# Band mask of each slot's first pair of heads written into PSUM by ScalarE, attended rows on two banks, and a few steps moved in the slot table

## The chip, the cores and the metric

One core of one Trainium2 chip. The time is device microseconds (us) of one execution. PE is the TensorE, DVE the VectorE, ACT the ScalarE, POOL the GpSimd, SP the engine that here only issues DMAs. Each has its own queue and works it in order; they meet at semaphores.

## The reference

A transformer block on x of 8 x 512 x 256 (batch, tokens, features), in float32:

```python
h = _layernorm(x) * (1 + ca) + sa
x = x + ga * _L0_attn_ref(h, w_qkv, b_qkv, w_out, b_out)   # 16 heads of 16, band |i - j| <= 64
h = _layernorm(x) * (1 + cb) + sb
x = x + gb * _L0_ffn_ref(h, gate_w, gate_bias, w_gate, w_up, w_down)   # 64 experts, 8 per token
# in the attention:
scores = jnp.einsum('bhqd,bhkd->bhqk', q, k) * SCALE + mask
attn = jax.nn.softmax(scores, axis=-1)
out = jnp.einsum('bhqk,bhkd->bhqd', attn, v)
```

The feed-forward part routes every token to 8 of 64 experts (capacity 256 each) and adds the weighted expert outputs.

## The kernel before

**Stages.** After a start, the attended part runs over 8 batches (0 to 7), then a tail routes the last batch, then 64 experts run, then the sums are put together. Each batch takes 20 slots: slot = 5g + u, where g counts four groups of four heads ("quads") and u five blocks of 128 keys. u = 0 and u = 4 are the ends of the band, 128 queries wide for each head; u = 1 to 3 are 256 wide.

**A slot on PE.** For two pairs of heads p = 0, 1, `scoresT` writes transposed scores into bank `bST[m % 2]`, m = 10g + 2u + p, so p = 0 is always bank scoresT0 and p = 1 always scoresT1. It begins with a product of an identity and the band mask (L1002, `start=True`), on which two products of keys and queries are added (L1006). Between them stand `fills` (L980), the scores of a later quad for the row maxima; none stand in slots with u = 3. Then `values` (L1022) multiplies the attended weights of the slot before. `turn_m`, in slots with u = 3, turns the maxima of the next quad; ACT copies them (L784) and sends them by DMA into the queries (`Qs<-MT`), which the first `scoresT` of the next quad waits for.

**The others.** ACT takes `exp` of each bank (`exps`, L779). DVE takes the row maxima (`maxima`, L1249, 4 instructions in each slot that has fills).

**Stage work** is put into the slots by a table, `AT`, a number for each step. At a slot of batch b three batches are in work: b itself, the one before (`prev`: its output product, second norm, routing) and the next ones (their first norm, projections and splitting; a negative number n means slot 20 + n of two batches earlier). The steps that matter here:

- `load_x` (SP, slot 6): the DMA of x of batch b + 2 into the single buffer `xt`. SP's queue has ahead of it, in this batch, storing the split projections (`store`, L435, slots 1 and 3), zeroing (L406) and 12 loads of the stacked operands (`stack`, L353, slot 4).
- `stats` (DVE, slots 9 and 10): the norm statistics of `xt`, two halves (`a_stats`, L1213 and L1217). The first half waits for the DMA of `load_x`.
- `onT`, `op`, `x1` (PE and ACT, PE, DVE): turn the attended rows of `prev`, multiply by `wo`, add to x (L1281 and L1284). x plus the bias comes from POOL (`c_xb`, L613, slot 2).
- `stats2`, `c_rstd`, `xhat`, `norm2`, `h2T`: statistics of that sum (DVE), their roots (POOL, slot 5), normalising (ACT, L805, slot 6), scale and shift (DVE, two instructions of L1303, both in slot 7), turned by PE in slots 8 and 9 (L1070), each into the same bank stageC.
- POOL besides splits the projections (L596, L599, L604), scales the sum by the output gate (`c_xs`, L619, slot 11) and, from batch 2 on, sends 32 groups of rows to the experts' slots by indirect DMA (L642).

On DVE the order inside one slot is: maxima, split_m, route, key, norm_o, `a_stats`, `a_mod`, `a_v`, `c_x1`, `c_stats`, `c_norm`.

Of the kernel before, what the change touches and what calls it, by code (L numbers as in the profile page):

```python
# [29 lines left out]
P = 128  # L30
# [33 lines left out]
    exp=10 * QUADS, pv=10 * QUADS, oTs=QUADS, oTp=QUADS, rec=QUADS, on=QUADS,  # L64
# [61 lines left out]
def build(nc, x, w_qkv, b_qkv, w_out, b_out, gate_w, gate_bias, w_gate, w_up, w_down, c, wmod, out):  # L126
    with ExitStack() as ctx:
# [613 lines left out]
        def _(act):  # L741
# [78 lines left out]
            def body(prev, now, nxt):  # L820
                for slot in range(SLOTS):
# [16 lines left out]
                    for k in at("onT", slot) if prev else []:  # L838
                        c_onT(prev, k)
# [60 lines left out]
        def _(pe):  # L900
# [304 lines left out]
        def _(dve):  # L1205
# [224 lines left out]
            def body(prev, now, nxt):  # L1430
                for slot in range(SLOTS):
# [146 lines left out]
```

## Time and profile before

| | |
|---|---|
| time, median of 3 runs | 989.44 us (984.01 to 989.56) |
| the profiled execution: time, span | 989.2 us, 987.5 us |
| busy: PE, DVE, ACT, POOL | 73%, 55%, 38%, 65% of the span |
| attended slots | 52.3 to 588 us |
| tail, experts, final sums | 588 to 690, 690 to 946, 946 to 987.5 us |

The profile is one execution, and times in its rows are from the span's start. A row of windows has the stretch, its length, the busy time and count of instructions of PE, PE's weight loads, DVE, ACT and POOL, then the granted clock of TensorE as a share of 2.4 GHz, the busy share of the DMA engines and GB/s. In a timeline the brackets at a row's end give the idle time ahead of it and what ended it.

### The profile page before, as it was taken

How to read it: one execution, taken by the hardware profiler on the slowest of the kernel's cores; microseconds unless marked ns; L12 is line 12 of the kernel's file. 1: busy time of each engine (PE TensorE's matmuls, PEld its weight loads, DVE VectorE, ACT ScalarE, POOL GpSimd, SP SyncE). 2: the span in 40 equal slices, each digit the busy share in tenths (PEclk: the TensorE clock that was granted, in tenths of full speed). 3: DMA queues.
4: the chain of work that ended last, by engine and by line, in shares of the span. 5: the costliest groups of instructions: out<-in, count | busy, mean ns of one | idle time of the engine just before them, and what ended most of it. 6: DMA issues, size and time to landing. Idle time of an engine off the chain costs nothing.

```text
span 987.5 us, 15482 instructions
## 1 busy us (share of the span) xinstructions
PE 719.3 (73%) x4732; PEld 470.7 (48%) x4732; DVE 544.6 (55%) x1974; ACT 373.7 (38%) x827; POOL 643.2 (65%) x592
## 2 busy tenths in 40 slices
PE   4579998997997897989988861200899998888200
PEld 3235555554554564554455530200788777666100
DVE  3566569779869878778678772600222222222038
ACT  2135654544444455445444530000344333333100
POOL 5206332687786886886885656776388888887630
PEclk9879998998987998898898976555899999999755
DMA  8695996275466446534526379100999999898878
GB/s 306 162 341 159 333 336 189 82 251 180 172 202 227 151 157 212 181 101 162 172 97 201 115 227 282 37 5 4 247 277 276 263 231 159 162 161 182 216 211 332
DMA packets 165134, 191.60 MB, mean 194 GB/s; under 512 B 21497, under 2 KB 146581, under 8 KB 165052
## 3 DMA queue, kind: packets, MB, share of 16 engines
q1 hardware_dynamic: 128636, 134.27, 42.7%
q0 software_dynamic: 30720, 38.03, 18.8%
q10 hardware_dynamic: 5696, 18.30, 5.2%
q8 instruction: 39, 0.64, 0.3%
q14 instruction: 43, 0.35, 0.1%
HBM read 100.77 MB, written 110.67 MB: 214 GB/s over the span
## 4 chain that ended last, share of the span: by engine, by line
PE 36%; DVE 20%; POOL 15%; DMA 12%; issue 11%; SPq 3%; ACT 2%; POOLq 0%; DVEq 0%; ACTq 0%
POOL acc_d L725 8%; DMA acc_d<-ys,xg 7%; PE stageA L952 6%; POOL slots_d L642 5%; PE outT L1022 4%; PE scores L980 4%; PE scoresT L1181 4%; DVE junk L1249 4%; PE scoresT L1002 4%; PE scoresT L1006 3%; PE stageA L962 2%; DVE pairs L1313 2%; PE stageC L1077 2%; DVE sc L1313 1%; PE stageC L1059 1%
## 5 line engine op out<-in xcount | busy, mean ns | idle before, releaser
L642 POOL DMA_INDIRECT slots_d<-H,dest x256 | 259.1, 1012 | 95.0 <-issue 57.4
L725 POOL DMA_INDIRECT acc_d<-ys,xg x128 | 198.4, 1550 | 60.3 <-issue 29.8
L1249 DVE CUSTOM_DVE_ANT_0 junk<-scores,mask 128x256 bf16<-128x256 f32 x512 | 187.6, 419 | 76.1 <-PE scores L980 75.8
L779 ACT ACTIVATE PT<-scoresT 128x512 f32<-128x512 f32 (+1 forms) x320 | 152.8, 508 | 140.7 <-PE scoresT L1006 137.1
L1181 PE MATMUL scoresT<-xgT,wgu 128*128 128x256 f32 x512 | 127.6, 393 | 23.0 <-ACT xgT L873 22.8
L1002 PE MATMUL scoresT<-mask,identb 128*128 128x512 bf16 (+1 forms) x320 | 116.5, 364 | 19.8 <-DMA Qs<-MT 14.3
L980 PE MATMUL scores<-Ks,Qs 96*128 96x256 bf16 x512 | 108.5, 298 | 30.4 <-DVE mrowmax L1249 26.6
L1181 PEld LDWEIGHTS scoresT<-xgT,wgu 128*128 128x128 f32 x512 | 96.1, 194 | 48.3 <-ACT xgT L873 35.3
L1006 PE MATMUL scoresT<-Qs,Ks 98*128 98x256 bf16 (+1 forms) x640 | 117.1, 267 | 0.0
L1022 PE MATMUL outT<-PT,Va 128*32 128x256 f32 (+1 forms) x1280 | 94.9, 370 | 0.0
L596 POOL TENSOR_TENSOR r<-p,parts 128x512 f32<-128x512 f32 x32 | 39.3, 1227 | 78.7 <-ACT parts L771 77.2
L1006 PEld LDWEIGHTS scoresT<-Qs,Ks 98*128 98x128 bf16 x640 | 66.9, 104 | 41.7 <-issue 12.5
L1532 DVE COPY xgT<-stageA 128x256 f32<-128x256 f32 x32 | 13.6, 424 | 122.4 <-PE stageA L1169 122.4
L952 PE MATMUL stageA<-hT,wqkv 128*128 128x512 f32 x128 | 74.0, 707 | 3.4 <-ACT p L767 2.4
L980 PEld LDWEIGHTS scores<-Ks,Qs 96*128 96x128 bf16 x512 | 45.9, 104 | 43.8 <-DVE mrowmax L1249 34.9
L1169 PE MATMUL scores<-ident,xg 128*128 128x128 f32 x128 | 24.9, 277 | 52.0 <-DMA xg<-slots_d 52.0
L1002 PEld LDWEIGHTS scoresT<-mask,identb 128*128 128x128 bf16 x320 | 33.0, 103 | 48.1 <-DMA Qs<-MT 20.7
L1532 DVE COPY xgT<-stageC 128x256 f32<-128x256 f32 x32 | 13.6, 424 | 75.8 <-PE stageC L1169 75.8
L886 ACT ACTIVATE ys<-outT,xg 128x256 f32<-128x256 f32 x64 | 26.8, 470 | 63.1 <-DMA acc_d<-ys,xg 56.6
L873 ACT ACTIVATE xgT<-scores 128x256 f32<-128x256 f32 x64 | 24.7, 386 | 67.3 <-PE scores L1169 67.3
L962 PE MATMUL stageA<-wqkv,hT 128*128 128x256 f32 x160 | 41.0, 395 | 9.0 <-DVE Va L1232 8.1
L886 ACT ACTIVATE ys<-turns,xg 128x256 f32<-128x256 f32 x64 | 26.8, 470 | 53.5 <-DMA acc_d<-ys,xg 47.0
(195 smaller groups left out, 1179.5 us busy)
## 6 DMA issues: line engine op xcount, KB each, us to landing
xg<-slots_d SPq DMA_DIRECT2D x64, 324.0 KB, 4.4
slots_d<-blank ACTq DMA_DIRECT2D x26, 648.0 KB, 5.1
parts_d<-parts SPq DMA_DIRECT2D x32, 384.0 KB, 2.7
Qs<-parts_d SPq DMA_DIRECT2D x96, 128.0 KB
Ks<-parts_d SPq DMA_DIRECT2D x90, 128.0 KB
acc_d<-zero SPq DMA_DIRECT2D x32, 272.0 KB
wgu<-L_ffn_w_gate_dram SPq DMA_DIRECT2D x64, 128.0 KB, 3.2
wgu<-L_ffn_w_up_dram SPq DMA_DIRECT2D x64, 128.0 KB, 3.3
```

Source lines behind the costliest of these rows:

```text
L642: pool.indirect_dma_start(out=slots_d[:, :], in_=H2[bt.par][:, t, :], in_offset=None, out_offset=bass.IndirectOffsetOnAxis(ap=dest[bt.par] ...
L725: pool.indirect_dma_start(out=acc_d[ACC[e]][:, :], in_=ys[e % NY][:, h, :], in_offset=None, out_offset=bass.IndirectOffsetOnAxis(ap=xg[e % ...
L779: sc_.activation(PT[m % NPT][:, :, 0:w], src, ACT.Exp).then_inc(sems["exp"], 1)
L886: sc_.activation(ys[e % NY][:, h, :], yb[:, h * D:(h + 1) * D], ACT.Copy, scale=xg[e % NX][:, h, D + e:D + e + 1]).then_inc(mo["yc"], 1)
L952: last = mm(bA[:, :], wqkv[:, k, f * P:(f + 1) * P], hT[:, k, BAND:BAND + S], start=(k == 0), stop=(k == C - 1))
L962: last = mm(bA[:, i * D:(i + 1) * D], hT[:, k, u * P:(u + 1) * P], wqkv[:, k, 2 * D:3 * D], start=(k == 0), stop=(k == C - 1))
L980: last = mm(bS[n % 2][:, i * 2 * P:(i + 1) * 2 * P], q[0:MROW, h, t * P:(t + 1) * P], kk[0:MROW, h, t * P:(t + 2) * P], start=True, stop=True)
L1002: mm(bST[m % 2][:, 0:2 * (hi - lo)].rearrange("p (h q) -> p h q", h=2), identb[:], half.unsqueeze(1).to_broadcast([P, 2, hi - lo]), start= ...
L1006: last = mm(bST[m % 2][:, i * (hi - lo):(i + 1) * (hi - lo)], kk[0:KROWS, h, u * P:(u + 1) * P], q[0:KROWS, h, lo:hi], start=False, stop=T ...
L1022: last = mm(bO[32 * j:32 * j + 32, lo:hi], Va[bt.par][rows, u, HQ * g + j, :], PT[m % NPT][rows, i, 0:hi - lo], start=(u == 0), stop=(u == ...
L1181: last = mm(bST[par][:, a * CAP:(a + 1) * CAP], wgu[e % NW][:, a, k, :], xgT[par][:, k, :], start=(k == 0), stop=(k == C - 1))
L1249: ins = v.tensor_tensor_reduce(out=junk[:, i, :], in0=bS[n % 2][:, i * 2 * P:(i + 1) * 2 * P], in1=mask[:, edge, :], scale=1.0, scalar=TAK ...
```

## The change

Three edits come together.

1. **Seeds.** For p = 0 the mask product is gone. ACT writes the band mask (a bf16 tile in SBUF, broadcast over two heads) into bank scoresT0 by a copy (`seed`), right behind the `exp` that emptied the bank and ahead of the `exp` of p = 1. The first product of keys and queries of the next slot waits for the semaphore `seed` in place of `exp`, and adds to what is there. A product of the identity over the whole bank, in the start, comes ahead of the first seed. p = 1 keeps its mask product.
2. **Two banks.** `onT`, `op` and `x1` of a batch that is not the last use stageC for the first half and stageA for the second (`PAIR`), so the waits of the second half for the first are gone. `a_proj` of the third projection, and `onT`, have waits in their place.
3. **The table.** `onT` moves from slots 2, 3 to 2, 2; `op` from 4, 5 to 3, 3; `x1` from 4, 5 to 3, 4; `stats2` from 5, 5 to 4, 5; `norm2` from 7, 7 to 7, 8; the first half of `stats` from slot 9 to slot 8.

```diff
-    load_x=(-14,), stats=(-11, -10), a_rstd=(-9,), ...
+    load_x=(-14,), stats=(-12, -10), a_rstd=(-9,), ...
-    xb=(2,), onT=(2, 3), op=(4, 5), x1=(4, 5), ..., stats2=(5, 5), c_rstd=(5,), xhat=(6,), norm2=(7, 7),
+    xb=(2,), onT=(2, 2), op=(3, 3), x1=(3, 4), ..., stats2=(4, 5), c_rstd=(5,), xhat=(6,), norm2=(7, 8),
...
+        PAIR = (bC, bA)
...
+            def seed(bt, m):
+                u = m % 10 // 2
+                half = mask[:, 1, P:2 * P] if u == 0 else mask[:, 1, 0:P] if u == U - 1 else mask[:, 1, :]
+                w = P if u in (0, U - 1) else 2 * P
+                if bt.b > 0 or m >= 2:
+                    after(act, "exp", bt, m - 1)
+                sc_.activation(bST[m % 2][:, 0:2 * w].rearrange("p (h q) -> p h q", h=2),
+                               half.unsqueeze(1).to_broadcast([P, 2, w]), ACT.Copy).then_inc(sems["seed"], 1)
...
                 sc_.activation(PT[m % NPT][:, :, 0:w], src, ACT.Exp).then_inc(sems["exp"], 1)
+                if p == 0 and m + 2 < 10 * QUADS:
+                    seed(bt, m + 2)
+                elif p == 0 and bt.b < B - 1:
+                    seed(batch(bt.b + 1), 0)
...
+                if j == 2 and bt.b >= 2:
+                    after(pe, "t1", batch(bt.b - 2), 2)
...
-                after(pe, "exp", bt, m - 1)
...
-                mm(bST[m % 2][:, 0:2 * (hi - lo)].rearrange("p (h q) -> p h q", h=2), identb[:],
-                   half.unsqueeze(1).to_broadcast([P, 2, hi - lo]), start=True, stop=False, skip_group_check=True)
+                if p == 0:
+                    after(pe, "seed", bt, m // 2 + 1)
+                else:
+                    after(pe, "exp", bt, m - 1)
...
+                    mm(bST[1][:, 0:2 * (hi - lo)].rearrange("p (h q) -> p h q", h=2), identb[:],
+                       half.unsqueeze(1).to_broadcast([P, 2, hi - lo]), start=True, stop=False, skip_group_check=True)
...
-                if bank is bC and k == 0:
+                if bt.b < B - 1 and bank is bC:
                     after(pe, "key", bt, -1)
-                elif bank is bC:
-                    after(pe, "onT", bt, k)
+                elif bt.b < B - 2:
+                    after(pe, "p32", batch(bt.b + 2), 2)
...
-                if bank is bC:
-                    after(pe, "t1", bt, n)
...
+            mm(bST[0][:, :], identb[:], mask[:, 0:2, :], start=True, stop=True).then_inc(s_pe0, 1)
```

Line numbers of the kernel after are higher: L1303 before is L1328 after, L1213 is L1238, L1249 is L1274, L1002 is L1025, L1006 is L1029, L1059 is L1082.

DVE, slots 7 to 9 of batch 3 (the same in batches 1 to 5). Before: the two steps of the second norm, then the maxima of slot 9, then the statistics of `xt`.

```order
L1303 TENSOR_TENSOR H2_0<-H2_0,mr 128x4x256 [waits s_xn2]
L1303 TENSOR_TENSOR H2_0<-H2_0,mr 128x4x256 [waits s_h2]
L1249 ISA junk,mrowmax<-scores0,mask 128x256 [waits s_smax,s_m2,s_Sp]
L1249 ISA mrowmax 128x1
L1249 ISA junk,mrowmax<-scores0,mask 128x256 [waits s_smax]
L1249 ISA mrowmax 128x1
L1249 ISA junk,mrowmax<-scores1,mask 128x256 [waits s_smax,s_Sp]
L1249 ISA mrowmax 128x1
L1249 ISA junk,mrowmax<-scores1,mask 128x256 [waits s_smax]
L1249 ISA mrowmax 128x1
L1213 BN_STATS stats<-xt 128x6 [waits x_loaded_odd]
```

After, the same place:

```order
L1328 TENSOR_TENSOR H2_0<-H2_0,mr 128x4x256 [waits s_xn2]
L1238 BN_STATS stats<-xt 128x6 [waits x_loaded_odd]
L1238 BN_STATS stats<-xt 128x6
L1242 BN_AGGR mv<-stats 128x2 [waits s_stats,s_rstd]
L1242 BN_AGGR mv<-stats 128x2 [waits s_stats]
L1328 TENSOR_TENSOR H2_0<-H2_0,mr 128x4x256 [waits s_h2]
L1274 ISA junk,mrowmax<-scores0,mask 128x256 [waits s_smax,s_m2,s_Sp]
L1274 ISA mrowmax 128x1
```

The first half of the statistics, with its wait for the load of x, now stands between the two steps of the second norm and ahead of the maxima of slot 9. PE's first `h2T` needs both steps of the norm.

DVE, slots 4 and 5 of batch 1, where `x1` and `stats2` stand. Before:

```order
L1281 TENSOR_TENSOR x1<-stageC,mr 128x512 [waits s_xb,s_op]
L1284 TENSOR_TENSOR x1<-x1,xc 128x512 [waits s_t1]
L1249 ISA junk,mrowmax<-scores0,mask 128x256 [waits s_smax,s_Sp]
L1249 ISA mrowmax 128x1
L1249 ISA junk,mrowmax<-scores0,mask 128x256 [waits s_smax]
L1249 ISA mrowmax 128x1
L1249 ISA junk,mrowmax<-scores1,mask 128x256 [waits s_smax,s_Sp]
L1249 ISA mrowmax 128x1
L1249 ISA junk,mrowmax<-scores1,mask 128x256 [waits s_smax]
L1249 ISA mrowmax 128x1
L1281 TENSOR_TENSOR x1<-stageC,mr 128x512 [waits s_xb,s_op]
L1284 TENSOR_TENSOR x1<-x1,xc 128x512 [waits s_t1]
```

After, from the end of slot 2 on:

```order
L1285 SCALAR_TENSOR_TENSOR M2<-mrowmax,M2 128x16 [waits s_m2]
L1306 TENSOR_TENSOR x1<-stageC,mr 128x512 [waits s_xb,s_op]
L1309 TENSOR_TENSOR x1<-x1,xc 128x512 [waits s_t1]
L1274 ISA junk,mrowmax<-scores0,mask 128x256 [waits s_smax,s_m2,s_Sp]
L1274 ISA mrowmax 128x1
L1274 ISA junk,mrowmax<-scores0,mask 128x256 [waits s_smax]
L1274 ISA mrowmax 128x1
L1274 ISA junk,mrowmax<-scores1,mask 128x256 [waits s_smax,s_Sp]
L1274 ISA mrowmax 128x1
L1274 ISA junk,mrowmax<-scores1,mask 128x256 [waits s_smax]
L1274 ISA mrowmax 128x1
L1306 TENSOR_TENSOR x1<-stageA,mr 128x512 [waits s_xb,s_op]
```

The first `x1` now comes ahead of the maxima of slot 4, where it came behind them.

ACT, slot 3 of batch 0. Before:

```order
L779 ACTIVATE PT2<-scoresT0 128x512 [waits s_pv,s_STp]
L779 ACTIVATE PT3<-scoresT1 128x512 [waits s_pv,s_STp]
L784 ACTIVATE MT<-turns 32x128 [waits s_mrow_ld,s_mTp]
L786 DMA Qs0<-MT 2x16x128 [waits s_mT]
L757 ACTIVATE hT<-stageA,mcol 128x512 [waits s_vp,s_mcol,s_hTp]
```

After:

```order
L791 ACTIVATE PT2<-scoresT0 128x512 [waits s_pv,s_STp]
L782 ACTIVATE scoresT0<-mask 128x256 [waits s_exp]
L791 ACTIVATE PT3<-scoresT1 128x512 [waits s_pv,s_STp]
L800 ACTIVATE MT<-turns 32x128 [waits s_mrow_ld,s_mTp]
L802 DMA Qs0<-MT 2x16x128 [waits s_mT]
```

A copy of the mask stands between the two `exp` of every slot; its width is that of the next slot.

## Rows read from the trace of the kernel before

**Rows 1.** Windows of batches 0 and 4 (columns as explained above).

```profile
52.32:116.89 64.57, 60.06 (x429) 31.82 (x429) 38.67 (x172) 34.55 (x70) 19.36 (x22) 0.94 0.78 274
...
322.96:391.95 68.99, 60.24 (x461) 36.18 (x460) 56.31 (x225) 34.45 (x71) 55.47 (x56) 0.93 0.56 184
```

**Rows 2.** Timeline of PE, slot 15 of batch 4.

```profile
371.92 0.28 PE L1002 MATMUL scoresT<-mask,identb 128*128 128x256 bf16 x1 [1.77 <-DMA Qs<-MT]
...
375.87 0.61 PE L980 MATMUL scores<-Ks,Qs 96*128 96x256 bf16 x2 [3.54 <-DVE mrowmax L1249]
```

**Rows 3.** Timeline of DVE, slot 12 of batch 4.

```profile
368.32 3.94 DVE L1313 TENSOR_TENSOR pairs<-pairs 128x64 f32<-128x64 f32 x4
```

**Rows 4.** Timeline of POOL, slot 11 of batch 4.

```profile
369.81 2.36 POOL L619 TENSOR_TENSOR x<-x,mr 128x1024 f32<-128x1024 f32 x1
```

**Rows 5.** The page, costliest groups: the mask product.

```profile
L1002 PE MATMUL scoresT<-mask,identb 128*128 128x512 bf16 (+1 forms) x320 | 116.5, 364 | 19.8 <-DMA Qs<-MT 14.3
```

**Rows 6.** Timeline of PE, slots 10 and 12 of batch 4: start us, us, what.

```profile
355.83 0.27 PE L1002 MATMUL scoresT<-mask,identb 128*128 128x256 bf16 x1
355.94 0.28 PE L1006 MATMUL scoresT<-Qs,Ks 98*128 98x128 bf16 x2
...
363.03 0.38 PE L1002 MATMUL scoresT<-mask,identb 128*128 128x512 bf16 x1
363.25 0.38 PE L1006 MATMUL scoresT<-Qs,Ks 98*128 98x256 bf16 x2
```

**Rows 7.** Timeline of ACT, a step that reads SBUF.

```profile
319.97 0.63 ACT L771 ACTIVATE parts<-p 128x512 bf16<-128x512 f32 x1
```

**Rows 8.** Timeline of PE, slot 1 of batch 4.

```profile
324.84 0.39 PE L1002 MATMUL scoresT<-mask,identb 128*128 128x512 bf16 x1 [0.47 <-ACT PT L779]
```

**Rows 9.** Timeline of the SP queue, batch 4.

```profile
345.75 3.86 SPq L353 DMA_DIRECT2D Ks<-parts_d  x6
349.65 0.64 SPq L416 DMA_DIRECT2D xt<-L_attn_x_dram  x1
```

**Rows 10.** Timeline of DVE, slots 7 to 9 of batch 4.

```profile
347.13 2.48 DVE L1303 TENSOR_TENSOR H<-H,mr 128x1024 f32<-128x1024 f32 x2 [0.76 <-ACT H L805]
...
355.75 0.75 DVE L1213 BATCH_NORM_STATS2 stats<-xt 128x6 f32<-128x256 f32 x2 [1.63 <-DMA xt<-L_attn_x_dram]
356.42 0.30 DVE L1217 BATCH_NORM_AGGREGATE mv<-stats 128x2 f32<-128x6 f32 x2
```

**Rows 11.** Timeline of PE, slots 8 and 9 of batch 4.

```profile
351.58 0.60 PE L1070 MATMUL stageC<-ident,H 128*128 128x128 f32 x4
352.01 0.27 PE L1002 MATMUL scoresT<-mask,identb 128*128 128x256 bf16 x1
```

**Rows 12.** Timeline of PE, slot 8 of batches 1 and 5 (first and last).

```profile
143.38 0.60 PE L1070 MATMUL stageC<-ident,H 128*128 128x128 f32 x4
...
422.10 0.60 PE L1070 MATMUL stageC<-ident,H 128*128 128x128 f32 x4
```

**Rows 13.** Timeline of DVE, slot 9 of batches 1 and 5 (first and last).

```profile
147.79 0.75 DVE L1213 BATCH_NORM_STATS2 stats<-xt 128x6 f32<-128x256 f32 x2 [1.86 <-DMA xt<-L_attn_x_dram]
...
424.57 0.75 DVE L1213 BATCH_NORM_STATS2 stats<-xt 128x6 f32<-128x256 f32 x2
```

**Rows 14.** Timeline of POOL, slot 19 of batch 3 to slot 2 of batch 4.

```profile
320.69 1.15 POOL L596 TENSOR_TENSOR r<-p,parts 128x512 f32<-128x512 f32 x1 [1.71 <-ACT parts L771]
...
332.76 2.36 POOL L613 TENSOR_TENSOR xc<-xc,gbo 128x1024 f32<-128x1024 f32 x1
...
336.31 1.17 POOL L604 TENSOR_TENSOR parts<-r,parts 128x512 bf16<-128x512 f32 x1
```

**Rows 15.** Timeline of DVE, slots 4 and 5 of batch 4.

```profile
336.03 2.01 DVE L1284 TENSOR_TENSOR x<-x,xc 128x512 f32<-128x512 f32 x1
...
340.06 0.69 DVE L1284 TENSOR_TENSOR x<-x,xc 128x512 f32<-128x512 f32 x1
```

**Rows 16.** Window: slots 15 and 16 of batch 4, behind a stop of PE.

```profile
375.90:382.00 6.10, 6.10 (x40) 3.62 (x41) 5.83 (x29) 2.17 (x4) 4.04 (x6) 0.56 0.69 224
```

More of the change, by code:

```diff
@@ L63 @@
     lpart=4, vp=3, v=3, Sp=8 * QUADS, smax=2 * 8 * QUADS, m2=2 * QUADS, mTp=QUADS, mT=QUADS, STp=10 * QUADS,
-    exp=10 * QUADS, pv=10 * QUADS, oTs=QUADS, oTp=QUADS, rec=QUADS, on=QUADS,
+    exp=10 * QUADS, seed=5 * QUADS, pv=10 * QUADS, oTs=QUADS, oTp=QUADS, rec=QUADS, on=QUADS,
     onTp=C, onT=C, op=2, t1=2, xb=2, x1=2, xs=1, stats2=T, aggr2=T, rstd2=4, xn2=T, h2=2, h2Tp=C, h2T=C,
@@ L72 @@
 AT = dict(
-    load_x=(-14,), stats=(-11, -10), a_rstd=(-9,), a_norm=(-6,), a_mod=(-9,), hT=(-4, -3), proj=(-2, -1, 7, 8),
+    load_x=(-14,), stats=(-12, -10), a_rstd=(-9,), a_norm=(-6,), a_mod=(-9,), hT=(-4, -3), proj=(-2, -1, 7, 8),
     split=(-1, 0, 0, 1, 1, 2, 8, 8, 9, 9, 10, 10), store=(1, 3, 10, 11), stack=(4, 12), v=(9, 11, 12),
-    xb=(2,), onT=(2, 3), op=(4, 5), x1=(4, 5), x1_store=(10,), xs=(11,), stats2=(5, 5), c_rstd=(5,), xhat=(6,), norm2=(7, 7),
+    xb=(2,), onT=(2, 2), op=(3, 3), x1=(3, 4), x1_store=(10,), xs=(11,), stats2=(4, 5), c_rstd=(5,), xhat=(6,), norm2=(7, 8),
     h2T=(8, 9), lg=(10,), route=(11, 12, 12, 13, 13, 14, 15, 15, 16, 17, 18, 18), cnt=(18,), key=(19,), zero=(3,),
@@ L440, in load_stack @@
                 if bt.b == 1:
-                    sp.wait_ge(s_pe0, 6)
+                    sp.wait_ge(s_pe0, 7)
                 if bt.b >= 2:
@@ L838, in body @@
                     for k in at("onT", slot) if prev else []:
-                        c_onT(prev, k)
+                        c_onT(prev, k, PAIR[k])
                     for _ in at("xhat", slot) if prev else []:
@@ L856, in _ @@
             load_side(act, batch(0), 0, 1)
+            act.wait_ge(s_pe0, 5)
+            seed(batch(0), 0)
             take_mT(batch(0), 0)
@@ L998, in scoresT @@
                 m = 10 * g + 2 * u + p
-                after(pe, "exp", bt, m - 1)
-                half = mask[:, 1, P:2 * P] if u == 0 else mask[:, 1, 0:P] if u == U - 1 else mask[:, 1, :]
-                mm(bST[m % 2][:, 0:2 * (hi - lo)].rearrange("p (h q) -> p h q", h=2), identb[:],
-                   half.unsqueeze(1).to_broadcast([P, 2, hi - lo]), start=True, stop=False, skip_group_check=True)
+                if p == 0:
+                    after(pe, "seed", bt, m // 2 + 1)
+                else:
+                    after(pe, "exp", bt, m - 1)
+                    half = mask[:, 1, P:2 * P] if u == 0 else mask[:, 1, 0:P] if u == U - 1 else mask[:, 1, :]
+                    mm(bST[1][:, 0:2 * (hi - lo)].rearrange("p (h q) -> p h q", h=2), identb[:],
+                       half.unsqueeze(1).to_broadcast([P, 2, hi - lo]), start=True, stop=False, skip_group_check=True)
                 for i in range(2):
@@ L1043, in c_onT @@
                 after(pe, "on", bt, QUADS)
-                if bank is bC and k == 0:
+                if bt.b < B - 1 and bank is bC:
                     after(pe, "key", bt, -1)
-                elif bank is bC:
-                    after(pe, "onT", bt, k)
+                elif bt.b < B - 2:
+                    after(pe, "p32", batch(bt.b + 2), 2)
+                elif bt.b == B - 2:
+                    after(pe, "v", batch(B), 0)
                 for t in range(T):
@@ L1114, in body @@
                     for k in at("onT", slot) if prev else []:
-                        c_onT(prev, k)
+                        c_onT(prev, k, PAIR[k])
                     for n in at("op", slot) if prev else []:
-                        c_op(prev, n)
+                        c_op(prev, n, PAIR[n])
                     for k in at("h2T", slot) if prev else []:
@@ L1411, in mod_gates @@
                 if part == 0:
-                    dve.wait_ge(s_pe0, 6)
+                    dve.wait_ge(s_pe0, 7)
                     v.tensor_copy(gates[:, 1, 0, :], bC[0:B, 0:D]).then_inc(s_v1, 1)
@@ L1452, in body @@
                     for n in at("x1", slot) if prev else []:
-                        c_x1(prev, n)
+                        c_x1(prev, n, PAIR[n])
                     for half in at("stats2", slot) if prev else []:
```

## The prediction

> **What bounds the kernel now.** I read the windows first, one for each attended batch. Batch 0, which has no second norm, no routing and no sends, takes 64.57 us of which PE is busy 60.06; batch 4, a full one, takes 68.99 with PE busy 60.24, DVE 56.31 and POOL 55.47 [rows 1]. POOL's sends have some 0.3 us between them that don't count as busy, so three in-order engines are nearly full and hand work to each other. Behind the attended slots come the tail and the experts. Neither is touched by the change, and both begin when the slots end, so the whole question is by how much the eight batches grow or shrink.
>
> Then I read the timeline of one full batch, engine by engine, to see who is late where. In batch 4 PE stands longest in slot 15: 1.77 us for the DMA of the maxima, then 3.54 us for DVE [rows 2]. DVE was late because four small `pairs` steps took 3.94 us together [rows 3] while POOL worked on `c_xs` for 2.36 us from 369.81 [rows 4].
>
> **What the seeds take away.** 160 of the 320 mask products go [rows 5]. A busy time of 0.38 us is not their price, since products overlap: the next one starts 0.22 us behind a wide one and 0.11 behind a narrow one [rows 6]. 96 wide and 64 narrow ones make 96 x 0.22 + 64 x 0.11 = 28 us of PE at full clock, 3.5 us in a batch. That is all there is to gain, and it comes only where PE is what the others wait for.
>
> **What they add.** A seed is a copy on ACT from SBUF. The nearest row is the 128x512 copy of L771, 0.63 us [rows 7]; a narrow one I take at half to two thirds of it. ACT is 34.45 us busy in 68.99 [rows 1], so 20 seeds of about 0.55, 11 us, fit beside its other work. What counts is latency: p = 0 of the next slot now waits for `exp` and a seed, and `exp` of p = 1 comes one seed later. Where PE already waits for ACT, as in slot 1 of batch 4 (0.47 us [rows 8]), p = 0 starts 0.6 us later and saves 0.22: a loss of 0.4. That is about one place in a batch. In slots with stage work behind them the seed is long done. Bounds for all seeds together: from 0 to 0.4 x 20 slots x 8 batches = 64 us; I take 0.4 in a batch, since the row shows one such place, and count it against the products below.
>
> **The table: one step decides.** `stats` of batch b + 2 moves from slot 9 to slot 8. Its load is not earlier: SP issued it at 349.65, right behind the twelve stack loads [rows 9]. Before, DVE finished both steps of the second norm at 347.13 + 2.48 = 349.61, did the maxima of slot 9, and then still had to wait 1.63 us for the load until 355.75 [rows 10]. After, the order is: first step of the norm, statistics, second step, maxima of slot 9. DVE therefore stands in slot 8 until 355.75; two statistics and their aggregates take until 356.65, the second step of the norm 1.24 (half of 2.48), so it is done at 357.9 [rows 10]. PE's first `h2T` needs it and started at 351.58, with slot 9 right behind at 352.01 [rows 11]. In batch 4 PE is held 357.9 - 351.6 = 6.3 us, and nothing else is queued on PE ahead of it.
>
> The same holds in batches 1 to 5, which have both a second norm and a batch + 2. In batch 1: 147.79 + 2.13 - 143.38 = 6.5 us; in batch 5: 424.57 + 2.13 - 422.10 = 4.6 us, at most, since there DVE came behind the load [rows 12, 13]. Batches 2 and 3 lie between, at 5.7 and 5.0. Sum of the five: 28 us. Batch 0 has no second norm and its load is there in time; batches 6 and 7 have no such statistics.
>
> Could what the change saves bring the load forward? It is tied to POOL, not to PE. POOL starts the splits of a batch when ACT hands over the first projection at 320.69, works without a gap worth the name through `c_xb` (332.76) and on to the split of 336.31 to 337.48 [rows 14]; the store, the zeroing and the twelve loads of SP follow back to back until 349.65 [rows 9]. From 320.69 to the landing it is 35 us, whatever PE does between. This also means that what PE saves in slots 19 to 8 of these batches is covered, and that what the new place of `x1` costs is covered too.
>
> **What `x1` costs.** The sum x1 needs `c_xb`, done at 335.12 [rows 14]. DVE now reaches it in slot 3 with the maxima of slot 4 queued behind, four of some 0.35. So after 335.12 DVE has 1.4 us more to do before the statistics of slot 5. In batches 1 to 5 the load hides that; in 6 and 7 it costs up to 1.4 each, against masks of 3.5 each.
>
> **Shared port.** DVE's addition of two SBUF tiles took 2.01 us at 336.03 and 0.69 at 340.06 [rows 15]; the first lay across POOL's split of 336.31 [rows 14]. The Trainium skill ("SBUF — State Buffer", section "SBUF: two separate sides") says that a DVE instruction with two SBUF inputs and a GpSimd one hold the shared pair for their whole length in turn. By that rule a norm step that meets a split would wait for all of it, which would make the sum up to 5 x 1.2 longer, 1020; the trace agrees in that the addition ended 0.56 us behind the end of that split. Without the rule: the second step of the norm, in its new place at 356.65, may take longer by as much as the addition did, 1.3 us. That is 0 to 1.3 in each of five batches, 0 to 6.5; I take 0 for the sum, since POOL's sends stand between its splits, and keep 6 for the range.
>
> **The clock.** In the stretch of 6.10 us behind PE's stop of 3.54 us, PE was busy all through at a granted clock of 0.56 [rows 2, 16], so 6.10 x 0.44 = 2.7 us were lost against full clock. The hold in slot 8 is longer than that stop and ends in slots 9 and 10, where PE, not DVE, sets the pace. Bounds 0 and 2.7; I take 2 in each of five batches: +10.
>
> **What comes back.** PE's two stops in slot 15 of batch 4 make 5.3 us [rows 2]. They arise because POOL lags and its long instructions fall on DVE's small ones [rows 3, 4]. POOL goes on while PE is held, so its lag shrinks by the hold, and `c_xs` then falls beside DVE's slot 11. I take 1.5 us back in each of batches 2 to 5: -6. Bounds 0 and the whole 5.3 in each.
>
> **The sum,** against the profiled execution, 989.2 us: hold +28; clock +10; stops -6; batch 0, where PE sets the pace, 3.5 less the seeds' latency, -3; mask products in slots 9 to 19 of batches 1 to 5, of which DVE, busy without a gap from slot 11, lets through 0.5 each, -2.5; batches 6 and 7, -2. Together +24.5: 1014 us. The profiled execution is the median of the runs shown to 0.2 us, so it stands for that too. The forecast's own range: without the clock term and with twice as much back from the stops, 998; with 2.7 of clock, the port and nothing back, 1029.
>
> **The rivals.**
> - **PE's relief counts in full and the hold does not.** It would need the load to be there before DVE gets to slot 8, by 6 us. For it: 28 us of products, twice that where the clock is 0.56. Against it: the wait of 1.63 us that DVE already had a slot later [rows 10]. It turns at a landing ahead of 349.6 in batch 4. With 16 to 20 us of the 28 it gives about 971. 8 in 100.
> - **The hold is given back later.** Had the stops of 5.3 us gone altogether in all five batches (27 us, of which I counted 6), the sum would be +24.5 - 21 = +3.5: 993. For it: DVE, which is late there, gets 6 us of standing in which POOL runs ahead. Against it: DVE stands too, so its own queue is no shorter, and its work from slot 11 on stays. 15 in 100.
> - **ACT joins in.** Seeds that delay both the next p = 0 and the `exp` of p = 1 in many short slots, 0.2 us over 100 slots, add 20: about 1034. For it: five engines in lockstep. Against it: ACT stands idle half of each batch. 11 in 100.
> - The edit does what it says: the products are gone from the order of PE. What it may not do is relieve anything, which is inside the forecast.
>
> **How the numbers follow.** Forecast (998 to 1029) 66 in 100, the three rivals 8, 15 and 11. The range of 990 to 1032 holds nearly all of the forecast, most of the second rival and half of the third, 8 in 10 together. Over 1% (9.9 us, about what a measurement of this kernel can tell from no change) slower: the third, nearly all of the forecast, 77 in 100. Within 1%: 15. Faster by more: 8.
>
> **What would show it.** In the profile after: DVE's first statistics of `xt` between the two steps of the second norm in batches 1 to 5, with 5 to 7 us of idle time before it that the load's DMA ended; PE idle ahead of L1093 by about as much; a granted clock near 0.5 in slots 9 and 10; a batch of some 74 us in place of 69 to 71, and batch 0 near 61.5. If those idle times are under 2 us, the forecast is wrong at its root. If they are there but the batch is under 71 us, the stops in slot 15 went with them.

## The result and the profile after

The changed kernel takes 1027.87 us (median of 4 runs, 1020.44 to 1028.69), the kernel before, run beside it, 986.73 (983.3 to 989.56). The ratio is 1.0402 with a 95% interval of 1.0336 to 1.0467: slower by 4%. The forecast was 1014, with a range of 990 to 1032.

The page of the kernel after, its span and its first part (busy time, share of the span, instructions), and two of its costliest groups:

```profile
span 1026.9 us, 15317 instructions
...
PE 735.7 (72%) x4572; PEld 473.2 (46%) x4573; DVE 543.8 (53%) x1974; ACT 450.2 (44%) x987; POOL 646.2 (63%) x592
...
L782 ACT ACTIVATE scoresT<-mask 128x512 f32<-128x512 bf16 (+1 forms) x160 | 82.5, 516 | 13.1 <-PE stageC L936 8.1
...
L1025 PE MATMUL scoresT<-mask,identb 128*128 128x512 bf16 (+1 forms) x160 | 65.7, 411 | 0.2
```

The edit did what it says: 160 mask products are left of 320 [rows 5], and ACT has 160 more instructions. PE is nevertheless busy longer than before (735.7 against 719.3 us), because what is left runs at a lower clock, 0.82 over the span against 0.86: one of the remaining mask products takes 411 ns on average, before 364 [rows 5]. The windows of batches 0 and 4 (columns as in [rows 1]):

```profile
50.23:116.31 66.08, 59.20 (x408) 30.33 (x409) 39.12 (x172) 43.84 (x90) 19.12 (x22) 0.91 0.75 268
345.69:423.64 77.95, 63.72 (x441) 36.94 (x440) 56.40 (x224) 43.99 (x91) 56.45 (x56) 0.85 0.49 163
```

Batch 4 is 9 us longer than its 68.99 [rows 1], of which only 3.5 are busy time of PE. Batch 0 is 1.5 us longer, where it should have been 3 shorter. The eight batches took 64.57, 64.92, 69.70, 71.45, 68.99, 71.49, 67.33 and 56.71 us before (the last one up to the end of its last `values`); after, 66.08, 73.48, 77.38, 78.52, 77.95, 75.98, 67.89 and 60.99. So nearly all of the loss, 37 of 39 us, lies in batches 1 to 5, where the forecast had put it. Batch 7 is 4.3 us longer, and what stands before batch 0 and behind batch 7 is 3.7 us shorter.

Where in the batch? The timeline of DVE, slots 7 and 8 of batch 4, answers to [rows 10]:

```profile
371.03 1.22 DVE L1328 TENSOR_TENSOR H<-H,mr 128x1024 f32<-128x1024 f32 x1
379.50 0.75 DVE L1238 BATCH_NORM_STATS2 stats<-xt 128x6 f32<-128x256 f32 x2 [7.25 <-DMA xt<-L_attn_x_dram]
380.17 0.30 DVE L1242 BATCH_NORM_AGGREGATE mv<-stats 128x2 f32<-128x6 f32 x2
380.39 1.19 DVE L1328 TENSOR_TENSOR H<-H,mr 128x1024 f32<-128x1024 f32 x1
```

DVE has half of the norm behind it, stands 7.25 us for the load of x, takes the statistics, and only then does the other half. In batches 1, 2, 3 and 5 it stands 5.04, 5.66, 5.42 and 3.03 us at the same place. PE, same stretch (it answers to [rows 11]):

```profile
375.13 1.94 PE L972 MATMUL stageA<-hT,wqkv 128*128 128x512 f32 x4
381.63 1.12 PE L1093 MATMUL stageC<-ident,H 128*128 128x128 f32 x4 [4.56 <-DVE H L1328]
```

PE's first `h2T` waits 4.56 us for that other half, and everything behind it with it. Once released it runs at a low clock: four transposes take 1.12 us where they took 0.60 [rows 11]. The load was where the forecast had it. SP's queue and the POOL step that starts the batch's splits (it answers to [rows 9, 14]):

```profile
343.52 1.15 POOL L598 TENSOR_TENSOR r<-p,parts 128x512 f32<-128x512 f32 x1 [1.47 <-ACT parts L773]
```

```profile
369.52 3.85 SPq L355 DMA_DIRECT2D Ks<-parts_d  x6
373.42 0.62 SPq L418 DMA_DIRECT2D xt<-L_attn_x_dram  x1
```

From 343.52 to the landing at 379.50 it is 36.0 us; before, 320.69 to 355.75, 35.1. Nothing that PE saved brought the load forward.

Two further readings speak of the seeds and of slot 15. PE in slots 1, 12, 15 and 16 of batch 4 (answers to [rows 2, 8]):

```profile
348.19 0.39 PE L1029 MATMUL scoresT<-Qs,Ks 98*128 98x256 bf16 x2 [1.21 <-ACT scoresT L782]
...
400.63 2.07 PE L982 MATMUL stageA<-wqkv,hT 128*128 128x256 f32 x4 [3.65 <-DVE Va L1257]
...
407.61 0.28 PE L1029 MATMUL scoresT<-Qs,Ks 98*128 98x128 bf16 x2 [1.55 <-DMA Qs<-MT]
409.79 0.39 PE L1029 MATMUL scoresT<-Qs,Ks 98*128 98x256 bf16 x2 [0.81 <-ACT scoresT L782]
```

Slot 1 now waits 1.21 us for a seed where it waited 0.47 for the exponentials [rows 8]. In slot 15 the stop of 3.54 us for DVE [rows 2] is gone; what is left is the wait for the maxima's DMA. But slot 12 has a stop of 3.65 us for DVE's `Va`, where before it was 0.88. DVE and POOL show where both come from:

```profile
393.77 3.26 DVE L1338 TENSOR_SCALAR ex<-ex 128x256 f32<-128x256 f32 x1
...
403.00 1.01 DVE L1338 TENSOR_TENSOR pairs<-pairs 128x64 f32<-128x64 f32 x4
```

```profile
394.51 2.36 POOL L621 TENSOR_TENSOR x<-x,mr 128x1024 f32<-128x1024 f32 x1
```

POOL's `c_xs` now ends 6 us ahead of the small `pairs` steps, which take 1.01 us together. Before, the two lay on each other and the same four steps took 3.94 us, from 368.32 to 372.26, while `c_xs` ran from 369.81 to 372.17 [rows 3, 4]. Now `c_xs`, from 394.51 to 396.87, lies on another step of DVE instead: `ex`, 0.29 us at 361.65 before, takes 3.26 and ends at 397.03. It stands in DVE's order ahead of `Va`, for which PE waits in slot 12. So in batch 4 the stop moved from slot 15 to slot 12. Over batches 1 to 5 slot 12 is 8.9 us longer than before and slots 15 and 16 are 10.0 shorter.

### The profile page after: what moved, and what is told of

It reads as the page before. It is cut to its first block, busy times and chain, and to the rows that moved or that the text cites. A ratio compares the mean times of both kernels' runs of the same rounds, so it can differ in the third digit from the quotient of the medians.

```text
span 1026.9 us, 15317 instructions
## 1 busy us (share of the span) xinstructions
PE 735.7 (72%) x4572; PEld 473.2 (46%) x4573; DVE 543.8 (53%) x1974; ACT 450.2 (44%) x987; POOL 646.2 (63%) x592
## 4 chain that ended last, share of the span: by engine, by line
PE 29%; DVE 17%; DMA 16%; POOL 16%; issue 11%; SPq 7%; ACT 4%; ACTq 0%; POOLq 0%; DVEq 0%
DMA acc_d<-ys,xg 9%; POOL acc_d L727 6%; SPq L355 6%; POOL slots_d L644 5%; DMA xt<-L_attn_x_dram 4%; PE outT L1045 3%; PE scoresT L1206 3%; PE scoresT L1029 3%; PE stageA L972 3%; DVE junk L1274 3%; PE scores L1000 3%; PE stageA L982 2%; PE stageC L1100 2%; PE scoresT L1025 2%; DVE sc L1338 2%
## 5 line engine op out<-in xcount | busy, mean ns | idle before, releaser
L1274 DVE CUSTOM_DVE_ANT_0 junk<-scores,mask 128x256 bf16<-128x256 f32 x512 | 189.2, 420 | 75.7 <-PE scores L1000 73.6
L791 ACT ACTIVATE PT<-scoresT 128x512 f32<-128x512 f32 (+1 forms) x320 | 160.5, 502 | 123.2 <-PE scoresT L1029 118.8
L1029 PE MATMUL scoresT<-Qs,Ks 98*128 98x256 bf16 (+1 forms) x640 | 130.2, 291 | 29.1 <-DMA Qs<-MT 15.5
L1000 PE MATMUL scores<-Ks,Qs 96*128 96x256 bf16 x512 | 116.7, 316 | 23.6 <-DVE mrowmax L1274 22.2
L1029 PEld LDWEIGHTS scoresT<-Qs,Ks 98*128 98x128 bf16 x640 | 64.6, 111 | 93.6 <-issue 34.8
L1045 PE MATMUL outT<-PT,Va 128*32 128x256 f32 (+1 forms) x1280 | 105.3, 407 | 0.0
L598 POOL TENSOR_TENSOR r<-p,parts 128x512 f32<-128x512 f32 x32 | 39.9, 1247 | 83.0 <-ACT parts L773 80.8
L782 ACT ACTIVATE scoresT<-mask 128x512 f32<-128x512 bf16 (+1 forms) x160 | 82.5, 516 | 13.1 <-PE stageC L936 8.1
L1557 DVE COPY xgT<-stageA 128x256 f32<-128x256 f32 x32 | 13.6, 425 | 122.1 <-PE stageA L1194 122.1
L972 PE MATMUL stageA<-hT,wqkv 128*128 128x512 f32 x128 | 68.8, 663 | 3.4 <-ACT p L769 2.4
L1000 PEld LDWEIGHTS scores<-Ks,Qs 96*128 96x128 bf16 x512 | 49.2, 111 | 40.4 <-DVE mrowmax L1274 31.1
L1025 PE MATMUL scoresT<-mask,identb 128*128 128x512 bf16 (+1 forms) x160 | 65.7, 411 | 0.2
L982 PE MATMUL stageA<-wqkv,hT 128*128 128x256 f32 x160 | 47.9, 446 | 17.9 <-DVE Va L1257 17.0
L1557 DVE COPY xgT<-stageC 128x256 f32<-128x256 f32 x32 | 13.6, 425 | 76.2 <-PE stageC L1194 76.2
```

Of the source, the lines that this page charges most:

```text
L782: sc_.activation(bST[m % 2][:, 0:2 * w].rearrange("p (h q) -> p h q", h=2), half.unsqueeze(1).to_broadcast([P, 2, w]), ACT.Copy).then_inc( ...
L982: last = mm(bA[:, i * D:(i + 1) * D], hT[:, k, u * P:(u + 1) * P], wqkv[:, k, 2 * D:3 * D], start=(k == 0), stop=(k == C - 1))
L1000: last = mm(bS[n % 2][:, i * 2 * P:(i + 1) * 2 * P], q[0:MROW, h, t * P:(t + 1) * P], kk[0:MROW, h, t * P:(t + 2) * P], start=True, stop=True)
L1025: mm(bST[1][:, 0:2 * (hi - lo)].rearrange("p (h q) -> p h q", h=2), identb[:], half.unsqueeze(1).to_broadcast([P, 2, hi - lo]), start=True ...
L1029: last = mm(bST[m % 2][:, i * (hi - lo):(i + 1) * (hi - lo)], kk[0:KROWS, h, u * P:(u + 1) * P], q[0:KROWS, h, lo:hi], start=False, stop=T ...
L1045: last = mm(bO[32 * j:32 * j + 32, lo:hi], Va[bt.par][rows, u, HQ * g + j, :], PT[m % NPT][rows, i, 0:hi - lo], start=(u == 0), stop=(u == ...
```

## The experiments

The theory on the stand was the hold: a late load in front of the norm's second step. Its rival: the seeds' latency on ACT, since slot 1 and batch 0 looked worse than forecast. All ratios are against runs of the kernel before made beside them on the same chip (medians 988.6 us for experiments 1 to 4, 988.2 for 5 to 8, 987.8 for 9 to 11). A difference between two experiments is one of medians and carries the uncertainty of both; the intervals are 2 to 6 us either way.

**1. Statistics back in slot 9.**

```diff
-    load_x=(-14,), stats=(-12, -10),
+    load_x=(-14,), stats=(-11, -10),
```

> The changed kernel with one number of the table put back: the first two statistics of a batch stand in slot 9 again, behind both steps of the second norm. Seeds, two banks and the rest of the table stay. If the wait for the load on DVE in slot 8 carries the loss (the traces: batches 1 to 5 are 37 us longer in all, DVE stands 5.04, 5.66, 5.42, 7.25 and 3.03 us in slot 8), PE's waits there go and 25 us or more of the 41 between the two kernels come back: 985 to 1003. If the seeds' latency on ACT carries it (slot 1 waits 1.21 us for a seed in place of 0.47 for the exponentials; batch 0, which has no such hold, is 1.5 us longer where it should be 3 shorter), at most 14 come back: 1013 or more.

Measured: 1003.86 us, ratio 1.0168 (1.0127 to 1.0209). One number of a table gives 24 us back. The hold is the largest part, but 15 us are left that it doesn't explain.

**2. The load two slots earlier instead.**

```diff
-    load_x=(-14,), stats=(-12, -10),
+    load_x=(-16,), stats=(-12, -10),
```

> The changed kernel with the load of x two slots earlier in SP's order, ahead of the stack loads; the statistics stay in slot 8. If the late load is the cause, DVE finds its tile there, the hold goes and the time is 985 to 1003, as with the statistics in slot 9, and perhaps below it, since DVE has the statistics behind it sooner. If the place of the statistics itself costs (their own DVE time ahead of the norm's second step, 0.9 us), or the seeds do, it stays at 1010 or more. A load ahead of the stack loads could also make these late and show up as a wait in slots 12 to 15 for the maxima's DMA.

Measured: 1003.24 us, ratio 1.0177 (1.0129 to 1.0225), the same as experiment 1. The timeline of DVE, slot 8 of batch 4:

```profile
356.49 1.22 DVE L1328 TENSOR_TENSOR H<-H,mr 128x1024 f32<-128x1024 f32 x1
357.62 0.74 DVE L1238 BATCH_NORM_STATS2 stats<-xt 128x6 f32<-128x256 f32 x2
358.50 1.19 DVE L1328 TENSOR_TENSOR H<-H,mr 128x1024 f32<-128x1024 f32 x1
```

The order is that of the changed kernel and there is no wait. So the statistics ahead of the norm cost nothing that shows; the wait for their load does. The time lies just above the upper end of what I expected, as that of experiment 1 did, again with 15 us unexplained.

**3. No seeds, the rest of the change kept.**

```diff
-                if p == 0 and m + 2 < 10 * QUADS:
-                    seed(bt, m + 2)
...
-                if p == 0:
-                    after(pe, "seed", bt, m // 2 + 1)
-                else:
-                    after(pe, "exp", bt, m - 1)
-                    ... mm(bST[1][...], identb[:], half, start=True)
+                after(pe, "exp", bt, m - 1)
+                ... mm(bST[m % 2][...], identb[:], half, start=True)
```

> The changed kernel with the mask again as a product for both pairs of heads, no seeds on ACT; two banks and the new table stay. If the hold carries the loss, it stays slower than before by 25 us or more: 1010 to 1028, and slot 8 of batch 4 still waits about 4 us for DVE. If the seeds' latency carries it, 27 us or more come back: 1000 or less.

Measured: 1023.51 us, ratio 1.0369 (1.0327 to 1.0411). The rival falls as the main cause: without any seed the kernel is 4 us faster (not clear of noise), not 27. PE waits 2.40 us for `H` in slot 8 of batch 4, less than the 4 I expected, and 16.7 us in batches 1 to 5 together, against 16.2 in the changed kernel.

**4. Seeds alone** (one bank, old table).

```diff
-        PAIR = (bC, bA)
+        PAIR = (bC, bC)
-    stats=(-12, -10), ... onT=(2, 2), op=(3, 3), x1=(3, 4), stats2=(4, 5), norm2=(7, 8)
+    stats=(-11, -10), ... onT=(2, 3), op=(4, 5), x1=(4, 5), stats2=(5, 5), norm2=(7, 7)
... and the waits of `a_proj`, `onT` and `op` as before
```

> The kernel before with the seeds alone: one bank and the old table. If the hold carries the loss, this is within 10 us of the kernel before, 978 to 998, with slot 8 of batch 4 free of a wait for DVE. If the seeds carry it, it is 1010 or more. Batch 0 should be about 66 us long, as in the changed kernel, against 64.6 before, if the seeds are what lengthens it.

Measured: 996.02 us, ratio 1.009 (1.0057 to 1.0123). The seeds are a loss by themselves, 7.4 us. Batch 0 took 64.2 us in its profiled run, not 66, so that part of my reading of the changed kernel was wrong. What the loss looks like, in slots 1 and 2 of batch 5, on ACT and on PE:

```profile
394.75 0.36 ACT L791 ACTIVATE PT<-scoresT 128x256 f32<-128x256 f32 x1
395.14 0.60 ACT L782 ACTIVATE scoresT<-mask 128x512 f32<-128x512 bf16 x1
```

```profile
395.80 0.39 PE L1027 MATMUL scoresT<-Qs,Ks 98*128 98x256 bf16 x2 [1.22 <-ACT scoresT L782]
```

The exponentials come late, behind the projection's two copies, and the seed of 0.60 us stands behind them. The windows from slot 1 of batch 5 on, seeds alone (slots 1 and 2) and then the kernel before (the same and 1.1 us of slot 3), with us, PE busy, PEclk, DMA share, GB/s:

```profile
395.80:402.80 7.00, 6.83 (x42) 0.62 0.29 104
```

```profile
393.93:399.80 5.87, 5.87 (x54) 1.00 0.35 124
```

In this stretch the granted clock is 0.62, between the two levels of 1.2 and 2.4 GHz; before, at the same place, behind a stop of 0.47 us for the exponentials, it is 1.00. In batch 4 slots 1 and 2 took 2.38 and 2.27 us behind the same wait, in batch 5 2.86 and 4.17: the wait doesn't lower the clock each time. Of PE's waits for seeds in this run, 15.8 us in 13 places, 13.6 are in slots 1 and 8; slots 3, 11 and 16 have one each, in batch 0.

**5. Two banks alone** (no seeds, statistics in slot 9).

```diff
 the edit of experiment 3, and
-    load_x=(-14,), stats=(-12, -10),
+    load_x=(-14,), stats=(-11, -10),
```

> The changed kernel without seeds and with the statistics in slot 9: what is left of the change is the pair of banks and the earlier places of onT, op, x1 and stats2. The seeds alone cost 7 us over the kernel before, and the changed kernel with the statistics in slot 9 costs 15. If the parts add up, this is 8 us slower than before, 993 to 1001. If the banks cost only where seeds delay PE too, it is within 4 us of before, 985 to 992.

Measured: 998.51 us, ratio 1.0093 (1.0058 to 1.0128). So the banks with their table cost something too when the hold is away. DVE in slots 3 and 4 of batch 4:

```profile
337.92 0.69 DVE L1297 TENSOR_TENSOR x<-stageC,mr 128x512 f32<-128x512 f32 x1 [4.24 <-POOL xc L615]
338.64 2.06 DVE L1300 TENSOR_TENSOR x<-x,xc 128x512 f32<-128x512 f32 x1
340.63 0.41 DVE L1265 CUSTOM_DVE_ANT_0 junk<-scores,mask 128x256 bf16<-128x256 f32 x1
```

And PE in slots 5 and 6:

```profile
341.45 0.39 PE L994 MATMUL scores<-Ks,Qs 96*128 96x256 bf16 x2 [1.59 <-DVE mrowmax L1265]
...
345.06 0.61 PE L994 MATMUL scores<-Ks,Qs 96*128 96x256 bf16 x2 [1.03 <-DVE mrowmax L1265]
```

`x1` now stands in DVE's order ahead of the maxima of slot 4. It needs `c_xb`, which POOL gives when it gives it, and DVE stands 4.24 us with maxima behind it that PE waits for. The waits of DVE over the whole run: for POOL's `xc` it is 29.8 us in 6 places. One of them, of 8.6 us, is in the tail, and the kernel before has one of 8.8 there; the other five, 21.2 us, are in the attended slots, where it has none.

```profile
DVE x L1297 <- POOL xc L615: 29.8, 6, 8.6
```

PE's own waits don't account for the 10 us. In slots 5 to 7 of batches 1 to 5 they make 14.3 us; before, 10.0, all in slot 7. But there are now two stops in a row, and the granted clock in these slots is 0.73 where it was 0.85. No run here separates the clock from the rest.

**6. The hold alone,** on the kernel before.

```diff
-    stats=(-11, -10), ... norm2=(7, 7)
+    stats=(-12, -10), ... norm2=(7, 8)
```

> The kernel before with the two numbers of the table that make the hold: first statistics in slot 8, second step of the second norm behind them. If the hold stands on its own feet, it costs here what it gave back there, 20 to 30 us: 1008 to 1020, with PE waiting 4 to 6 us in slot 8 of batches 1 to 5. If it took the earlier x1 and the seeds to bring it out, it is under 1000.

Measured: 1023.05 us, ratio 1.0349 (1.0288 to 1.0409). Two numbers, 35 us, 3 above the range that I expected. PE in slot 8 of batch 4, and its waits over the whole run (us in total, times, longest):

```profile
377.83 1.11 PE L1070 MATMUL stageC<-ident,H 128*128 128x128 f32 x4 [6.23 <-DVE H L1303]
```

```profile
PE stageC L1070 <- DVE H L1303: 28.5, 5, 6.6
```

The five waits are 6.57, 5.99, 4.56, 6.23 and 5.16 us. Slots 8 and 9 of these batches took 38.4 us in all before and 77.2 here; less the waits that leaves 10.3 us which PE spent longer on the same work, its clock being 0.81 in the stretch behind the wait:

```profile
377.83:386.50 8.67, 8.66 (x66) 0.81 0.26 93
```

The five batches together are 30.5 us longer (377.1 against 346.6), so 8 us came back. That is a difference of larger numbers. Slots 14 to 16 of the five batches are 24 us shorter (slot 15 of batch 4 took 1.79 us in place of 5.92), but slot 12 is 8.5 us longer and slots 17 and 18 are 5.9 longer.

Set beside experiment 3, which has the banks and their table on top of this hold, the two are the same: 1023.51 and 1023.05 us, ratios 1.0369 and 1.0349. With the hold in place the banks cost nothing that shows.

**7. Seeds in 16 of 20 slots,** on experiment 4.

```diff
+        APART = (1, 8, 11, 16)
...
             def seed(bt, m):
+                if m // 2 in APART:
+                    return
...
-                if p == 0:
+                if p == 0 and m // 2 not in APART:
...
```

> The kernel before with seeds in 16 of 20 slots: slots 1, 8, 11 and 16, where PE waited up to 1.2 us for one, have their product back. If those waits, and the clock of 0.7 behind the one in slot 1 (against 1.00 at the same place before), are what eats the products saved, this is 4 to 14 us below the seeds everywhere: 982 to 992, slots 1 and 2 again under 2.6 us in all batches. If the seeds cost by what ACT is late in all slots, it stays at 994 or more.

Measured: 989.87 us, ratio 1.0018 (0.9995 to 1.0041). With the products of the four bad places back the loss is gone, and slots 1 and 2 take 2.36 and 2.26 us in each of batches 1 to 6. No run took four other slots out for comparison. But there is no gain either, though 128 products are away, 64 wide and 64 narrow, by the pitches of [rows 6] 21 us of PE at full clock. The waits of PE, this kernel and then the kernel before:

```profile
PE scores L1000 <- DVE mrowmax L1274: 38.1, 22, 4.1
...
PE turns L1007 <- DVE M L1285: 14.7, 15, 3.4
...
PE stageA L982 <- DVE Va L1257: 9.6, 7, 2.1
```

```profile
PE scores L980 <- DVE mrowmax L1249: 26.6, 18, 3.9
...
PE turns L987 <- DVE M L1260: 11.9, 10, 3.6
...
PE stageA L962 <- DVE Va L1232: 8.1, 7, 1.9
```

PE waits 15.8 us more for DVE (62.4 against 46.6). By that estimate three quarters of the relief turned into waits for DVE.

**8. Both steps of the norm ahead of the late statistics.**

```diff
-    stats=(-12, -10), ... norm2=(7, 8)
+    stats=(-12, -10), ... norm2=(7, 7)
```

> The changed kernel with both steps of the second norm in slot 7, ahead of the statistics, which stay in slot 8 and wait there for the load as before. If the loss comes by way of the norm's second step, for which h2T and all of PE behind it wait, this is near the kernel with the statistics in slot 9: 1002 to 1012. If DVE's standing as such is what counts (the maxima of slot 9 behind it), it stays at 1018 or more.

Measured: 1001.2 us, ratio 1.0128 (1.0064 to 1.0191). DVE in slots 7 and 8 of batch 4, and PE's only wait for it in the next slots:

```profile
356.02 2.48 DVE L1328 TENSOR_TENSOR H<-H,mr 128x1024 f32<-128x1024 f32 x2
363.35 0.75 DVE L1238 BATCH_NORM_STATS2 stats<-xt 128x6 f32<-128x256 f32 x2 [4.85 <-DMA xt<-L_attn_x_dram]
```

```profile
365.12 0.39 PE L1000 MATMUL scores<-Ks,Qs 96*128 96x256 bf16 x2 [0.50 <-DVE mrowmax L1274]
```

DVE still stands 4.85 us for the same load, and it costs nothing that shows: experiment 1, where that wait is 0.21 us, took 1003.86. So the loss is not DVE's idle time but what was queued behind it, the one step that PE needs next.

**9. Two banks with `x1` where it was.**

```diff
 experiment 5, and
-    x1=(3, 4), stats2=(4, 5)
+    x1=(4, 5), stats2=(5, 5)
```

> The run with two banks alone (998.5), with x1 and its statistics back in slots 4 and 5; onT and op stay early, in two banks. If the loss of the banks comes from x1 ahead of the maxima of slot 4 (there DVE stood 4.24 us in batch 4 for POOL's xc, and PE 1.59 us for the maxima in slot 5), this is back at the kernel before: 984 to 992, and DVE's wait for POOL in slot 4 is under 2.5 us. If PE's own order costs (both op products in slot 3, 3.6 us in a row, ahead of the scores of the next slots), it stays at 995 or more.

Measured: 994.25 us, ratio 1.0059 (1.0033 to 1.0086). Neither: DVE's wait for POOL is back at 7.6 us in one place, but only some 4 of the 10 us came back, and the intervals of the two experiments overlap. PE's waits in slots 5 to 7 are as long as in experiment 5 (14.6 us in batches 1 to 5), at a clock of 0.82 in place of 0.73. So the share of `x1` is not clear of noise, and the rest lies in the early `onT` and `op` or in the waits that came with the two banks; which of them, and how, no run here shows.

**10. Experiment 7 and the load two slots earlier.**

```diff
-    load_x=(-14,)
+    load_x=(-16,)
```

> Seeds in 16 of 20 slots, one bank, old table, and the load of x two slots earlier, which takes DVE's remaining wait for it in slot 9 (1.63 us in batch 4) away. If that wait is on the path, up to 1.6 us in each of five batches come on top of the 990 measured without: 980 to 986. If PE is busy beside it, no change: 986 to 992.

Measured: 989.49 us, ratio 1.0012 (0.9992 to 1.0032). No change: DVE's waits for the load, 2.02, 1.64 and 1.97 us in three batches of experiment 7, are gone, and they were beside work of PE.

**11. Both ideas of the change, without the two waits and the four bad places.**

```diff
 the changed kernel with APART = (1, 8, 11, 16),
 stats=(-11, -10), x1=(4, 5), stats2=(5, 5)
```

> Seeds in 16 of 20 slots and two banks for onT and op in slots 2 and 3, with x1 where it was and the statistics in slot 9: every part of the change kept, without the two waits and without the four bad places. If the parts found make up the whole loss, it is within 5 us of the kernel before: 982 to 993. If something of the banks or the seeds remains, 995 or more.

Measured: 990.47 us, ratio 1.0034 (1.0012 to 1.0055). That repairs 37 us of the 39. Its interval lies just above 1, and no version here beats the kernel before.

## Why the prediction was right, and what in it was not

Direction, place and the mechanism of the hold were right; the sum was 15 us short (+24.5 against +39.4 of span), and the terms erred by more than the sum shows. The profiled executions give it by parts, each against the kernel before, in us of span:

| | forecast | changed kernel | experiment 6, hold alone | experiment 3, hold and banks |
|---|---|---|---|---|
| batches 1 to 5, slots 0 to 9 | +38 | +35.0 | +39.9 | +37.8 |
| batches 1 to 5, slots 10 to 19 | -8.5 | +1.8 | -9.4 | -6.2 |
| batch 0 | -3 | +1.5 | -1.6 | -0.6 |
| batches 6 and 7 | -2 | +4.8 | +2.1 | +3.5 |
| ahead of and behind the batches | 0 | -3.7 | -0.6 | -0.4 |
| together | +24.5 | +39.4 | +30.5 | +34.0 |

- **The hold.** Forecast 6.5, 5.7, 5.0, 6.3 and 4.6 us, 28 in all. Alone on the kernel before it was 6.57, 5.99, 4.56, 6.23 and 5.16, 28.5 in all. It could be read from before because both ends were in the trace: when the load lands, and when PE wants `h2T`.
- **The clock.** Forecast +10 over five batches; experiment 6 gives 10.3. It was sized from one stretch at 0.56 behind a stop of 3.54 us [rows 2, 16].
- **What comes back.** Forecast -6; experiment 6 gives -8, and that the two are near is in part luck. The forecast looked at slot 15 alone. There, in slots 14 to 16, 24 us came back, four times as much; and 14 were lost again in slots 12, 17 and 18, of which it said nothing. In the changed kernel slots 10 to 19 gave nothing back; they are 1.8 us longer. What it said of `c_xs` came about (in batch 4 it lies on the small `pairs` steps no more), but it fell on another DVE step instead, and the stop moved to slot 12. How much of the whole is due to `c_xs` no run here shows.
- **The shared port.** The prediction cited the Trainium skill ("SBUF — State Buffer", section "SBUF: two separate sides") for a DVE instruction with two SBUF inputs and a GpSimd one taking turns at a shared pair of ports. The trace agrees in the length: four `pairs` steps took 3.94 us beside `c_xs` and 1.01 without it, and the one that took 3.16 of this ended 0.10 us behind `c_xs`. The rule as it was cited doesn't cover `ex`, which reads one tile and was lengthened too. At the place where I weighed that rule, the norm's second step in its new place, it took 1.19 us in three batches and 1.68 and 1.76 in the other two: 1 us in all, where I took 0.
- **The parts don't add.** Hold, banks and seeds cost 34.9, 10.3 and 7.4 alone, 52.6 together, but 39.2 in company, and what each is worth depends on the order. Taking the statistics out first (experiment 1), then the banks (to experiment 4), then the seeds gives 24.0, 7.8 and 7.4. Putting the hold in first (experiment 6), then the banks (experiment 3), then the seeds gives 34.9, 0.5 and 4.4. The reason shows in slot 8: PE waits 28.5 us for `H` in experiment 6, 16.7 with the banks and 16.2 with banks and seeds. The banks make PE late for slot 8, and a late PE waits less; the seeds change little there.
- **`x1`.** "In batches 1 to 5 the load hides that", and in the sum it stood at nothing. For the changed kernel that was right: slots 0 to 9 of these batches are no longer with the banks than without them (+37.8 and +39.9), since `h2T` starts when the load has landed. What the prediction didn't say is that the cover goes with the hold. Without it the banks cost 10 us (experiment 5). I had counted DVE's work after `c_xb`, 1.4 us, and neither that DVE stands until then with maxima queued that PE needs, 4.24 us in a batch, nor a lower clock behind two stops in place of one.
- **The mask products, the term with the wrong sign.** Forecast -7.5 for batch 0, slots 9 to 19 and batches 6 and 7. The seeds cost 7.4 us alone and 4.4 in company (experiment 3 against the changed kernel, a difference not clear of noise), so this term alone was some 12 us off, most of what the sum was short. The latency per place was about right: 1.22 in place of 0.47 us, with 0.22 saved, is 0.5. But there are several such places, in slots 1 and 8 above all, not one in a batch, and I gave the clock behind them nothing: over slots 10 to 19 of batches 1 to 5 it is 0.92 in experiment 3 and 0.84 in the changed kernel. Slots 15 to 17 of batch 4, in the changed kernel, behind the waits of 1.55 and 0.81 us shown above, and then in experiment 3:

```profile
407.61:416.48 8.87, 7.89 (x64) 0.81 0.74 254
```

```profile
403.51:411.13 7.62, 6.93 (x66) 1.00 0.83 255
```

  And in the places without latency PE's saving turned into waits for DVE (experiment 7), which the prediction said of slots 11 on, but not of the rest.
- **The rivals.** The relief in full (971) and the stops given back altogether (993) didn't come. ACT joining in (1034) was partly true: not 0.2 us in a hundred slots, but a few places and a clock.

## What to carry to other kernels

Before moving a step up in an in-order queue, ask two questions: when does its input arrive, and what stands behind it that another engine needs. DVE's wait for one load cost the changed kernel 27 us with one step of the norm behind it, and nothing that shows with that step ahead of it (experiment 8). Work taken off an engine that takes its turn with two others is worth only what the next one lets through, and work moved to a third engine is worth less than nothing at each place where that engine already hands over late. And terms read from the trace of before, each by itself, are not to be added without asking whether one shortens the wait of another. Nor is a stop gone for good because its cause moved: look at what the cause falls on next.

## What the runs showed of the hardware

- ACT's copy of the mask from SBUF into PSUM takes 0.60 us for 128x512 and 0.39 for 128x256, the same as its exponentials out of PSUM (0.60 and 0.37).
- Behind a wait of PE of 1.22 us the granted clock was 0.62 over 7 us in batch 5 of experiment 4, and 1.00 in batch 4 behind the same wait. In slots 1 and 2 of the changed kernel, behind 1.21 or 1.22 us, it was 1.00 in batch 2, 0.74 in batches 3 and 4, and 0.61 and 0.58 in batches 5 and 6. In the forecast I had given a clock term to the hold alone.
- One DVE instruction was drawn out to 0.04 to 0.29 us behind the end of POOL's `c_xs` (2.36 us) in each of batches 1 to 5 of the changed kernel: `ex`, 128x256, took 3.26 us in batch 4 in place of 0.29, and `M`, 128x16, took 2.99 in batch 5 in place of 0.17. DVE's reciprocal of 128x256 took 1.75 us, with `c_xs` across its end (batch 2) and without it (batch 4).
